# Macaron block on one core: the maxima's rows on another queue, the causal mask of the transposed scores without its own matmuls, and score units spread over a step

## The chip, the cores and the metric

One of the eight cores of a Trainium2 chip runs the whole program. A core has five engines with a queue each: PE (TensorE, matmuls into PSUM), DVE (VectorE), ACT (ScalarE), POOL (GpSimd) and SP, which only issues DMAs and waits. The metric is the device time of one execution in microseconds. The profile is of one execution; its span runs from the first to the last recorded instruction.

## What is computed

Four sequences of 256 tokens, 512 features, in float32. The block is half a feed-forward network, attention, and half a feed-forward network again:

```
x = x + 0.5 * ffn(layernorm(x))
x = x + attn(layernorm(x))
x = x + 0.5 * ffn(layernorm(x))

ffn:  h = silu(x @ w_gate) * (x @ w_up); h @ w_down        (width 1376, weights in 4 bits, scaled by group)
attn: qkv = x @ Wqkv                                        (32 heads of 16; one k and one v for all heads)
      scores = q k^T / 4 + slope[head] * (pos_k - pos_q)    (-1e30 where pos_k > pos_q)
      out = softmax(scores) @ v @ Wo
```

## The kernel before

All instructions are placed by hand, each engine's stream in a block of its own; a stream runs in the order in which it is written, and streams meet at semaphores. There is no scheduler. The program has these parts:

- **Stage A** (s = 0): weights are dequantised and half of the tokens goes through the first network, 11 column tiles j (`NJ`), for each `gate_up`, `silu`, `h_mul`, `h_high`/`h_low` and `down`. Matrices are split into a high and a low part, and three products stand for one.
- **Stage B** (s = 1): the other half of the tokens. Between its 11 tiles lies the preparation of attention: masks, tables and slopes on DVE (`partition_masks`, `tables`, `slope_table`, all in j = 0), the layer norm of the first half (`moments`, `rstds`, in j = 1), transposes on PE (in j = 2), and the projections of sequences 0 and 1.
- **Attention**: for each sequence b (a "step 0" to "step 3" below) 12 sub-steps n, which pair with the units of 8 heads in three forms, `o, u = divmod(n, 3)`. In sub-step n of b the kernel computes the transposed, shifted scores of b (`shifted_scores`, keys on partitions, banks 4 and 5), their exponentials on ACT (`exps`, into `pt` and `pt_far`), and sums with v one group later (`near_values`, `far_values`, then `even_heads` on ACT, `odd_heads` on DVE, `swap_sums` on PE, `normalise` on DVE). At the same time it computes plain scores of sequence b + 1 (`scores`, banks 6 and 7) for the maxima alone (`maxima` on DVE): `score_units` gives one unit to sub-steps 0 and 1, two to sub-step 2, and so on up to 8. A unit's scores wait until the unit before has been reduced. `between` holds what else lies in a sub-step: in steps 0 and 1 the layer norm, k, v and q of sequence b + 2, from step 1 on the output projection of b - 1, in step 3 the transposes for the last network.
- **Stage C and D** (s = 2, 3): the last network.

The operand `qp[b]` of both score products holds, per half s of the partitions, 64 rows: q's parts, the slopes and, in rows 18 and 19, the maxima with their sign turned, so that the matmul subtracts them. It is filled by DMA, all on SP's queue: `q_to_dram(b)` writes q to DRAM, `q_to_rows(b)` brings first the 16 slope rows (2 DMAs), then, once q has arrived in DRAM, q's rows (6 DMAs, semaphore `q_in[b]`), and `max_to_rows(b)` the maxima from the tile `two` (4 DMAs of 16 KB, semaphore `m_in[b]`). `shifted_scores(b, 0)` waits for `m_in[b]`, and `scores(b + 1, 0)`, the next thing in PE's stream, for `q_in[b + 1]`. The order on SP's queue is:

```
q_to_rows(1)
max_to_rows(0)
...
q_to_dram(2)
q_to_rows(2)
max_to_rows(1)
sp.wait_ge(a_st, 2 * NU)
q_to_dram(3)
q_to_rows(3)
max_to_rows(2)
max_to_rows(3)
```

Both score products get the causal mask from matmuls of their own, a product of an identity with a triangle of -1e30 in bfloat16, which opens the accumulation in the bank: L1337 for the plain scores, L1373 for the transposed ones (two per unit, 256 columns for u < 2 and 512 for u = 2). GpSimd does nothing once stage B has begun, but for one copy, which widens the slopes to `qp_a` (L542), and the making of `kconst`.

## Time and profile before

| | us |
|---|---|
| median of three runs | 712.94 (708.77 to 724.35) |
| profiled execution | 708.63, of which the span is 706.8 |
| PE busy | 605.2 (86%) |
| DVE busy | 326.1 (46%) |
| ACT busy | 158.9 (22%) |
| GpSimd busy | 47.8 (7%) |

The mean granted clock of TensorE is 0.925 of full speed. Busy shares are means over stages with different limits: the two networks keep PE busy nearly all the time, attention (from about 258 to 511 us) doesn't. A row `a [b <-ENGINE tile Lnnn]` of the timeline means that the engine sat idle b us before it, and what released it. `SPq` and `ACTq` are the DMA issues on those engines.

### The profile page before, as it was taken

How to read it: one execution, taken by the hardware profiler on the slowest of the kernel's cores; microseconds unless marked ns; L12 is line 12 of the kernel's file. 1: busy time of each engine (PE TensorE's matmuls, PEld its weight loads, DVE VectorE, ACT ScalarE, POOL GpSimd, SP SyncE). 2: the span in 40 equal slices, each digit the busy share in tenths (PEclk: the TensorE clock that was granted, in tenths of full speed). 3: DMA queues.
4: the chain of work that ended last, by engine and by line, in shares of the span. 5: the costliest groups of instructions: out<-in, count | busy, mean ns of one | idle time of the engine just before them, and what ended most of it. 6: DMA issues, size and time to landing. Idle time of an engine off the chain costs nothing.

```text
span 706.8 us, 7705 instructions
## 1 busy us (share of the span) xinstructions
PE 605.2 (86%) x3064; PEld 425.8 (60%) x3064; DVE 326.1 (46%) x641; ACT 158.9 (22%) x284; POOL 47.8 (7%) x59
## 2 busy tenths in 40 slices
PE   2499999979999978880798589868699999999998
PEld 1387777868776754540454233323367888788886
DVE  6798998633124455441255354554531124421113
ACT  1332323111111122230123222333411111211111
POOL 5683000003000000000000000000000000000000
PEclk9999999999999995995789968879899999999999
DMA  6587110961935400009003800000029100100001
GB/s 203 180 257 233 45 37 13 307 284 31 152 87 70 51 4 1 1 30 146 7 1 90 93 1 1 1 5 1 1 85 344 33 0 1 59 1 1 0 1 59
DMA packets 36956, 51.54 MB, mean 73 GB/s; under 512 B 10188, under 2 KB 27446, under 8 KB 36504
## 3 DMA queue, kind: packets, MB, share of 16 engines
q1 hardware_dynamic: 32592, 40.39, 24.1%
q0 software_dynamic: 2656, 10.57, 4.6%
...
## 4 chain that ended last, share of the span: by engine, by line
PE 59%; DVE 6%; DMA 4%; ACT 2%; SPq 2%; issue 1%; ACTq 0%
PE bank L1262 22%; PE bank L1280 10%; PE bank L1423 4%; PE bank L1312 4%; PE bank L1345 4%; PE bank L1395 3%; PE bank L1337 3%; PE bank L1381 3%; DVE nm L1032 2%; PE bank L1373 2%; PE bank L1416 2%; DMA qp_b<-two 2%; PE bank L1232 1%; DMA qp_c<-two 1%; SPq L424 1%
## 5 line engine op out<-in xcount | busy, mean ns | idle before, releaser
L1280 PE MATMUL bank<-w_d,hs 128*128 128x512 f32 (+1 forms) x528 | 129.2, 394 | 2.8 <-DVE hs L877 1.3
L1280 PEld LDWEIGHTS bank<-w_d,hs 128*128 128x128 f32 (+1 forms) x528 | 98.0, 188 | 26.8 <-issue 4.3
L1032 DVE TENSOR_REDUCE nm<-bank 128x2 f32<-128x512 f32 (+1 forms) x96 | 61.8, 686 | 109.9 <-PE bank L1345 109.9
L871 DVE TENSOR_TENSOR hf<-sil,bank 128x512 f32<-128x512 f32 (+1 forms) x44 | 30.2, 686 | 168.7 <-PE bank L1262 168.6
L1262 PE MATMUL bank<-xt,w_far 128*128 128x512 f32 (+1 forms) x384 | 92.5, 395 | 0.0
L1262 PE MATMUL bank<-xt,w_mid 128*128 128x512 f32 x384 | 91.7, 395 | 0.0
L1262 PEld LDWEIGHTS bank<-xt,w_mid 128*128 128x128 f32 x384 | 73.2, 191 | 15.4
L1262 PEld LDWEIGHTS bank<-xt,w_far 128*128 128x128 f32 (+1 forms) x384 | 69.3, 181 | 18.2
L1262 PE MATMUL bank<-xt,w_near 128*128 128x512 f32 x288 | 71.7, 405 | 9.4 <-issue 9.4
L1262 PEld LDWEIGHTS bank<-xt,w_near 128*128 128x128 f32 x288 | 55.4, 195 | 22.9 <-issue 10.7
L1373 PE MATMUL bank<-ident_b,causal 128*128 128x256 bf16 (+1 forms) x96 | 24.9, 347 | 40.5 <-DMA qp_b<-two 22.4
L604 ACT ACTIVATE sil<-bank 128x512 f32<-128x512 f32 (+1 forms) x44 | 26.3, 597 | 141.1 <-PE bank L1262 141.0
L612 ACT CAST hs<-hf 128x512 fp32r<-128x512 f32 (+1 forms) x44 | 27.3, 621 | 130.2 <-DVE hf L871 130.2
L1373 PEld LDWEIGHTS bank<-ident_b,causal 128*128 128x128 bf16 x96 | 8.4, 107 | 56.3 <-DMA qp_b<-two 22.7
L877 DVE TENSOR_TENSOR hs<-hf,hs 128x512 fp32r<-128x512 f32 (+1 forms) x44 | 32.9, 747 | 20.0 <-ACT hs L612 19.9
L1232 PE MATMUL bank<-ident,xn 128*128 128x128 f32 x96 | 17.0, 325 | 24.0 <-DVE xn L804 19.9
L1337 PE MATMUL bank<-causal,ident_b 128*128 128x256 bf16 (+1 forms) x96 | 25.1, 347 | 14.2 <-DVE nm L1032 13.4
L1312 PE MATMUL bank<-xa,wqkv 128*128 128x256 f32 x128 | 34.8, 428 | 0.0
L656 ACT ACTIVATE pt_a<-bank 128x512 f32<-128x512 f32 x32 | 17.4, 595 | 75.7 <-PE bank L1381 75.7
L1087 DVE RECIPROCAL den<-bank 128x256 f32<-128x256 f32 x16 | 28.0, 1753 | 13.6 <-PE bank L1416 13.6
L1232 PEld LDWEIGHTS bank<-ident,xn 128*128 128x128 f32 x96 | 13.1, 167 | 28.8 <-issue 19.1
L656 ACT ACTIVATE pt_b<-bank 128x512 f32<-128x512 f32 x32 | 17.4, 594 | 57.3 <-PE bank L1381 57.3
...
## 6 DMA issues: line engine op xcount, KB each, us to landing
...
```

Of the source, the lines that this page charges most:

```text
L656: nc.scalar.activation(dst, src, ACT.Exp).then_inc(a_exp, 1)
L871: nc.vector.tensor_tensor(hf[0:jw(jt(s, p)), n % 2, :], sil[0:jw(jt(s, p)), n % 2, :], up_ps[0:jw(jt(s, p)), :], ALU.mult).then_inc(h_ok, 1)
L877: nc.vector.tensor_tensor(hs[0:jw(jt(s, p)), n % 2, 1, :], hf[0:jw(jt(s, p)), n % 2, :], hs[0:jw(jt(s, p)), n % 2, 0, :].bitcast(F32), ALU ...
L1032: nc.vector.tensor_reduce(nm[:, min(u, 1), 2 * h0 + s:2 * (h0 + heads) + s - 1:2], bank[6 + s][:, :].rearrange("p (h n) -> p h n", h=heads ...
L1232: ins = nc.tensor.transpose(ps[:, k * P:(k + 1) * P], xn[:, n % 2, k * P:(k + 1) * P], ident[:, :])
L1262: ins = nc.tensor.matmul(ps[0:jw(j), :], w_gu(a, k, gu, j), xt[:, b, k, :], start=(k == 0 and q == 0), stop=(k == KT - 1 and q == 2))
L1280: ins = nc.tensor.matmul(acc[t][:, :], hs[0:jw(j), n % 2, a, t * P:(t + 1) * P], w_d[0:jw(j), j, b, :], start=(p == 0 and q == 0), stop=(p ...
L1312: ins = nc.tensor.matmul(q_bank(b, h)[:, m * S:(m + 1) * S], wqkv[:, k, (2 * h + m) * P:(2 * h + m + 1) * P], xa[:, k, :], start=(k == 0), ...
L1337: nc.tensor.matmul(ps[:, :, 4 * P // heads - P:], ident_b[:, :], causal[:, :].unsqueeze(1).to_broadcast([P, heads, P]), start=True, stop=F ...
L1345: ins = nc.tensor.matmul(bank[6 + s][:, i * w:(i + 1) * w], qp[b][rows, h, min(u, 1) * P:(min(u, 1) + 1) * P], kp[rows, b % 3, 0:w], start ...
L1373: nc.tensor.matmul(ps[:, :, 0:P], causal[:, :], ident_b[:, :].unsqueeze(1).to_broadcast([P, heads, P]), start=True, stop=False, skip_group ...
L1423: ins = nc.tensor.matmul(out_bank(b, t)[:, :], normed(b)[:, k, t * P:(t + 1) * P], wo[:, k, :], start=(k == 0), stop=(k == KT - 1))
```

## The change

- `max_to_rows` moves from SP's queue to ACT's. ACT issues the four DMAs for sequence b + 1 at the end of sub-step 11 of b, behind the exponentials and `even_heads` of that sub-step; those for sequence 0 right before attention.
- The mask matmuls L1373 of the transposed scores go. In their place the operands `kp` and `qp` get eight step functions of 32 positions in rows that were free (`key_steps`, `steps`, `kconst`, `slope_rows` 4 to 11), by which the product itself gets -1e30 for whole blocks of 32, and GpSimd sets the rest to zero behind the exponentials, with one `affine_select` per unit (512 elements per partition for u < 2, 1024 for u = 2). `near_values` and `far_values` wait for it (`a_sel`). The preparation gets longer by some GpSimd and DVE instructions, and four more DMAs to `slope_rows`.
- Where a sub-step has two units of plain scores, the second now comes behind `between` on PE, and on DVE behind `odd_heads` and `normalise`.
- In stage B `moments` and `rstds` come in j = 0, and masks and tables in j = 1 behind the first normalised tiles.
- A small exponential is put ahead of `max_high(0)`, and a small Silu behind the last exponentials.
- In step 2 and 3 the output projection moves one sub-step later, and in step 3 the transposes for stage C one earlier, into banks 6 and 7 instead of 0 and 1, without the wait for `a_x` 6.

```diff
@@ sync
-            def max_to_rows(b):
-                sp.wait_ge(a_mhi, b + 1)
...
             q_to_rows(1)
-            max_to_rows(0)
             sp.wait_ge(up_ok, 2 * NJ)
             q_to_dram(2)
             q_to_rows(2)
-            max_to_rows(1)
@@ gpsimd
+            for b in range(B):
+                for n in range(NU):
+                    o, u = divmod(n, 3)
+                    pool.wait_ge(a_exp, 2 * (NU * b + n) + 2)
+                    if u < 2:
+                        p = pt[o % 2][:, 2 * u:2 * u + 2, :, 0:P].rearrange("p h s q -> p (h s) q")
+                    else:
+                        p = pt_far[:, :, :, :].rearrange("p h s q -> p (h s) q")
+                    nc.gpsimd.affine_select(out=p, in_=p, compare_op=ALU.is_ge, fill=0.0, base=0,
+                                            pattern=[[0, 4 if u < 2 else 8], [1, P]],
+                                            channel_multiplier=-1).then_inc(a_sel, 1)
@@ scalar
+            def max_to_rows(b):
+                act.wait_ge(a_mhi, b + 1)
+                act.wait_ge(a_mlo, b + 1)
+                act.wait_ge(q_in[b], 16 * 8)
...
+                        act.dma_start(qp[b][64 * s + 18 + r:64 * s + 19 + r, :, :].bitcast(F32),
+                                      two[s:NH:2, r, :].bitcast(F32)).then_inc(m_in[b], 16)
...
-                if j == NJ - 1:
-                    max_high(0)
+            act.wait_ge(hot_ok, 1)
+            nc.scalar.activation(hot[:, 0:1], hot[:, 1:2], ACT.Exp)
+            max_high(0)
+            max_to_rows(0)
...
+                if n == 11 and b + 1 < B:
+                    max_to_rows(b + 1)
@@ vector
                 if j == 0:
-                    partition_masks()
-                    tables()
-                    slope_table()
-                if j == 1:
                     dve.wait_ge(x_upd, 4)
                     moments(range(4))
                     rstds(0)
@@ tensor, shifted_scores
-                for s in range(2):
-                    ps = bank[4 + s][:, :].rearrange("p (h q) -> p h q", h=heads)
-                    nc.tensor.matmul(ps[:, :, 0:P], causal[:, :], ident_b[:, :].unsqueeze(1).to_broadcast([P, heads, P]),
-                                     start=True, stop=False, skip_group_check=True)
@@ tensor, near_values
-                pe.wait_ge(a_exp, 2 * (3 * g + 2))
+                pe.wait_ge(a_sel, 3 * g + 2)
@@ tensor, between
-                first = 7 if b == 1 else 4
+                first = 7 if b == 1 else 5
...
-                if b == B - 1 and n in (8, 10):
-                    if n == 8:
-                        pe.wait_ge(a_x, 6)
-                    for t in range(n - 8, n - 6):
+                if b == B - 1 and n in (7, 9):
+                    for t in range(n - 7, n - 5):
                         ffn_transposes(2, t)
@@ tensor, attention loop
-                        for k in score_units(b + 1, n):
-                            scores(b + 1, k)
+                    units = score_units(b + 1, n) if (b, n) != (0, 0) else ()
+                    for k in units[0:1]:
+                        scores(b + 1, k)
...
                     between(b, n)
+                    for k in units[1:2]:
+                        scores(b + 1, k)
```

PE's stream at the end of step 0 and the start of step 1, before (L1373 is the mask of the transposed scores, L1381 their product, L1337 and L1345 mask and product of the plain scores, L1416 `swap_sums`, L1395 `near_values`):

```order
L1373 MATMUL bank<-ident_b,causal 128x2x128 [waits exp_done,max_rows_placed1]
L1373 MATMUL bank<-ident_b,causal 128x2x128
L1381 MATMUL bank<-qp_b,kp 128x512 x2
L1337 MATMUL bank_7<-causal,ident_b 128x512 [waits max_lo_ready,k_rows_ready,q_rows_placed2]
L1337 MATMUL bank_7<-causal,ident_b 128x512
L1345 MATMUL bank_7<-kp,qp_c 128x128 x8
L1416 MATMUL bank<-den,swap 128x256 [waits attn_normed,odd_heads_added]
L1395 MATMUL bank<-pt_b,vp 32x256 [waits odd_heads_added,exp_done]
```

The same place now (L1439 is the product of the transposed scores, L1399 and L1407 the plain scores, L1474 `swap_sums`, L1453 `near_values`):

```order
L1439 MATMUL bank<-qp_b,kp 128x512 [waits exp_done,max_rows_placed1]
L1439 MATMUL bank<-qp_b,kp 128x512
L1399 MATMUL bank_7<-causal,ident_b 128x512 [waits max_lo_ready,k_rows_ready,q_rows_placed2]
L1399 MATMUL bank_7<-causal,ident_b 128x512
L1407 MATMUL bank_7<-kp,qp_c 128x128 x8
L1474 MATMUL bank<-den,swap 128x256 [waits attn_normed,odd_heads_added]
L1453 MATMUL bank<-pt_b,vp 32x256 [waits odd_heads_added,exp_masked]
```

The two mask matmuls are gone; the wait for q's rows of sequence 2 stands where it stood, right behind the first transposed scores, and `near_values` waits for the select.

ACT's stream around the end of step 0, before (L656 `exps`, L642 `max_high`, L666 `even_heads`):

```order
L642 CAST two<-bank_7 32x256 [waits k_rows_ready,max_transposed]
L656 ACTIVATE pt_far<-bank 128x4x128 [waits shifted_scores_t_done,all_keys_times_v]
L656 ACTIVATE pt_far<-bank 128x4x128 [waits shifted_scores_t_done]
L666 ACTIVATE num<-bank,pmask 128x256 [waits sums_swapped,attn_normed,all_keys_times_v]
L666 ACTIVATE den<-bank,pmask 128x256
L656 ACTIVATE pt_a<-bank 128x2x256 [waits shifted_scores_t_done,first_keys_times_v]
```

And now (L690 `exps`, L666 `max_high`, L700 `even_heads`, L675 `max_to_rows`):

```order
L666 CAST two<-bank_7 32x256 [waits k_rows_ready,max_transposed]
L690 ACTIVATE pt_far<-bank 128x4x128 [waits shifted_scores_t_done,all_keys_times_v]
L690 ACTIVATE pt_far<-bank 128x4x128 [waits shifted_scores_t_done]
L700 ACTIVATE num<-bank,pmask 128x256 [waits sums_swapped,attn_normed,all_keys_times_v]
L700 ACTIVATE den<-bank,pmask 128x256
L675 DMA qp_b<-two 1x16x256 [waits q_rows_placed1,max_lo_ready,max_hi_ready]
L675 DMA qp_b<-two 1x16x256 x3
```

The four DMAs stand behind one sub-step's exponentials and copies, where SP issued them as soon as `two` was ready, but for what lay ahead of them on its own queue.

PE's stream in sub-step 2 of step 1, before (two units of plain scores one behind the other, then L1312, half of a q projection) and now (L1374 between them):

```order
L1337 MATMUL bank_7<-causal,ident_b 128x2x128 [waits max_ready]
L1337 MATMUL bank_7<-causal,ident_b 128x2x128
L1345 MATMUL bank_7<-kp,qp_c 128x256 x4
L1337 MATMUL bank_7<-causal,ident_b 128x512 [waits max_ready]
L1337 MATMUL bank_7<-causal,ident_b 128x512
L1345 MATMUL bank_7<-kp,qp_c 128x128 x8
L1312 MATMUL bank<-xa,wqkv 128x256 [waits attn_xt_ready]
L1312 MATMUL bank<-xa,wqkv 128x256 x3
```

```order
L1407 MATMUL bank_7<-kp,qp_c 128x256 x4
L1374 MATMUL bank<-xa,wqkv 128x256 [waits attn_xt_ready]
L1374 MATMUL bank<-xa,wqkv 128x256 x3
L1399 MATMUL bank_7<-causal,ident_b 128x512 [waits max_ready]
L1399 MATMUL bank_7<-causal,ident_b 128x512
L1407 MATMUL bank_7<-kp,qp_c 128x128 x8
```

The second unit moved behind the projection.

## Rows read from the trace of the kernel before

**Rows 1.** Windows over attention: length, busy time (count) of PE to POOL, clock, DMA share, GB/s.
```profile
257.70:326.50 68.80, 49.65 (x310) 28.62 (x309) 33.82 (x70) 18.93 (x37) 0.00 (x0) 0.77 0.15 31
...
340.20:399.35 59.15, 53.73 (x353) 29.69 (x352) 29.36 (x46) 16.88 (x35) 0.00 (x0) 0.90 0.28 46
...
406.50:461.75 55.25, 47.33 (x290) 20.26 (x290) 27.87 (x41) 15.73 (x33) 0.00 (x0) 0.78 0.01 1
461.75:511.30 49.55, 36.02 (x235) 15.68 (x235) 25.39 (x50) 19.57 (x39) 0.00 (x0) 0.84 0.01 2
```

**Rows 2.** Chain of waits between steps 0 and 1.
```profile
316.35 4.10 DMA q_rows<-qst
...
326.52 13.04 DMA qp_b<-two
...
340.94 0.54 PE bank L1337
```

**Rows 3.** Timeline of PE from the end of step 0: start, us, what, idle before it.
```profile
339.61 0.61 PE L1373 MATMUL bank<-ident_b,causal 128*128 128x256 bf16 x2 [22.36 <-DMA qp_b<-two]
...
356.39 1.03 PE L1337 MATMUL bank<-causal,ident_b 128*128 128x512 bf16 x2 [1.38 <-DVE nm L1032]
```

**Rows 4.** Windows where q's rows of sequences 2 and 3 end, columns as in rows 1.
```profile
337.00:337.50 0.50, 0.00 (x0) 0.00 (x0) 0.00 (x0) 0.00 (x0) 0.00 (x0) 0.50 0.34 29
...
404.00:404.50 0.50, 0.00 (x0) 0.00 (x0) 0.00 (x0) 0.00 (x0) 0.00 (x0) 0.50 0.48 39
```

**Rows 5.** Timeline of SP's queue.
```profile
315.95 0.84 SPq L402 DMA_DIRECT2D q_rows<-qst  x2
...
382.93 0.82 SPq L402 DMA_DIRECT2D q_rows<-qst  x2
```

**Rows 6.** Timeline of PE in steps 2 and 3.
```profile
407.77 1.04 PE L1337 MATMUL bank<-causal,ident_b 128*128 128x512 bf16 x2
...
453.23 1.22 PE L1416 MATMUL bank<-den,swap 128*128 128x256 f32 x2 [1.11 <-DVE den L1076]
...
495.55 1.85 PE L1232 MATMUL bank<-ident,xn 128*128 128x128 f32 x8 [3.47 <-DVE x L1094]
```

**Rows 7.** Chain of waits in step 2.
```profile
412.87 0.54 PE bank L1373 x2
...
461.75 2.17 DMA qp_a<-two
```

**Rows 8.** Timeline of ACT at the end of step 2.
```profile
461.70 0.49 ACT L666 ACTIVATE den<-bank,pmask 128x256 f32<-128x256 f32 x1
```

**Rows 9.** Chain of waits at the end of step 1.
```profile
390.53 0.22 PE bank L1373 x2
```

**Rows 10.** Chain of waits of step 3, its shares by line.
```profile
by line: PE bank L1395 13.3%; PE bank L1423 12.1%; PE bank L1381 10.5%; PE bank L1416 8.9%; PE bank L1373 8.6%; PE bank L1232 6.5%; issue 5.8%; ACT pt_far L656 5.8%; DMA qp_a<-two 4.6%; DVE den L1087 3.7%; DVE den L1076 3.6%; PE bank L1406 
```

**Rows 11.** Timeline of POOL.
```profile
1.54 0.29 POOL L467 TENSOR_SCALAR_AFFINE_SELECT ident<-ident 128x128 f32<-128x128 f32 x1 [0.16 <-POOL slope_in L465]
...
167.32 3.61 POOL L542 CAST qp_a<-slope_in 128x4096 fp32r<-128x4096 f32 x1 [44.66 <-PE bank L1262]
...
171.61 1.04 POOL L549 TENSOR_SCALAR kconst<-kconst,pmask 128x256 f32<-128x256 f32 x1
```

**Rows 12.** Timeline of DVE in stage B, j = 3 and 4.
```profile
168.23 3.25 DVE L877 TENSOR_TENSOR hs<-hf,hs 128x512 fp32r<-128x512 f32 x1 [0.69 <-ACT hs L612]
...
181.47 0.69 DVE L877 TENSOR_TENSOR hs<-hf,hs 128x512 fp32r<-128x512 f32 x1 [0.69 <-ACT hs L612]
```

**Rows 13.** Timeline of PE in stage B, j = 2.
```profile
139.67 2.88 PE L1262 MATMUL bank<-xt,w_mid 128*128 128x512 f32 x12
146.29 1.06 PE L1232 MATMUL bank<-ident,xn 128*128 128x128 f32 x8 [3.74 <-DVE xn L804]
147.12 4.58 PE L1262 MATMUL bank<-xt,w_mid 128*128 128x512 f32 x12
```

**Rows 14.** Chain of waits at the start of attention: start, us, what.
```profile
262.71 1.28 ACT L656
```

100 lines of the change are left out of this document (72 added, 28 removed).

## The prediction

> **What bounds the kernel now.** I read the page first (which engine is busy, and in which slices), then the windows over attention, then the chain of waits inside each step, and last the timelines of single engines around each wait. In the two networks PE runs nearly without a gap, and the change hardly touches them. In attention it doesn't: in its four steps PE is busy 49.7, 53.7, 47.3 and 36.0 us of 68.8, 59.2, 55.3 and 49.6 [rows 1], and the granted clock is 0.77 to 0.90, a mix of the two levels 1.2 and 2.4 GHz. Inside a step the chain runs mostly through PE; between steps it runs through a DMA. The largest wait of the program is there: between steps 0 and 1 q goes to DRAM in 4.10 us, SP issues q's rows, and the maxima's rows, four small DMAs behind them on the same queue, take 13.04 us to land, until 339.56 [rows 2]. PE waits 22.4 us for them [rows 3], and again at the same place between steps 1 and 2.
>
> **The change part by part.**
>
> *Maxima's rows on ACT's queue.* This looks like it could give back these waits. It can't, because of what PE does next. Right behind the first transposed scores its stream has the plain scores of the next sequence, which wait for all of q's rows, and this wait has stayed in its place. Those rows move as long as the DMA engines are busy, to about 337.4, and in the next gap to about 404.3 [rows 4]. SP started with them at 315.95 and 382.93 [rows 5], so they arrive 21.4 us later. Before, PE reached those plain scores at 340.94 and 407.77 [rows 2, 6], which is 25.0 and 24.8 us behind the same starts. The gain is 25.0 - 21.4 = 3.6 and 24.8 - 21.4 = 3.4; I take 0.3 off each for the maxima's 64 KB in between, and count 3.3 + 3.1 = 6.4 us. The first transposed scores then lie inside the wait. As the lag of 21.4 us starts at the last q of the step, whatever makes the step faster behind that point (sub-steps 10 and 11 of step 0, 7 to 11 of step 1) is worth nothing.
>
> Between steps 2 and 3 there is no q, and the same edit costs. The last DMA left SP at 461.75 and took 2.17 us [rows 7]. On ACT all four come behind the last exponentials and a copy that ends at 462.19 [rows 8]; with about 0.6 us for each of three issues ahead of it (the lag of SP's own, estimated) the last leaves at 464.0 and lands at 466.1 instead of 463.9: 2.2 later, of which the missing mask matmul returns 0.3. Cost 1.9 us. Ahead of step 0 ACT is idle, and nothing changes.
>
> The Trainium skill ("DMA: Bandwidth & Descriptors", "Issuing engines are not separate DMA queues") says that a second issuing engine saves little more than issue time, since all transfers run on the same 16 DMA engines; its section on queues and rings says that each engine takes turns between the queues it has work for. By the first, the maxima's rows would land with q's rows and the 6.4 us would be gone (a rival below); by the second they overtake. No row here shows two queues at once.
>
> *Mask matmuls gone.* There are 96. What counts is their part of the chain: a pair with 256 columns is 0.22 us there at full clock [rows 9], so 0.43 with 512, and 0.54 at half clock [rows 7]. In step 0 four pairs are on the path ahead of the last q (sub-steps 4, 5, 7, 8): 0.22 + 0.43 + 0.22 + 0.43 = 1.3; the first three sub-steps wait for DVE. In step 1 there are four as well (1, 2, 4, 5): 1.3, and some of it at half clock, 1.6. In step 2 sub-steps 1, 2, 4 and 10 stand at half clock, 5, 7 and 8 at full: 0.54 + 0.5 + 0.54 + 0.43 + 0.43 + 0.22 + 0.43 = 3.1. In step 3, where PE waits for exponentials and these for the masked scores, they are 8.6% of the chain's 47.4 us [rows 10], 4.1.
>
> *Select on GpSimd.* The nearest row is a select of 128 elements in 0.29 us [rows 11]; with 0.1 as its fixed part, 512 elements take 0.9 and 1024 take 1.6, or 3.4 us per group of three sub-steps, which last 10 to 14. By the slowest rate in sight, 1.04 us for 256 elements [rows 11], it is 2.1 and 4.2, 8.4 per group. Both fit, and `near_values` and `far_values` come a sub-step or more behind the exponentials, some 4 to 5 us; so I price the wait at nothing, with that cover. It can touch DVE: beside the copy L542 on GpSimd a DVE subtraction took 3.25 us, and 0.69 without it [rows 12]. In attention one DVE instruction per group, the product in `normalise`, has two SBUF operands, and step 3 has some more. It follows `swap_sums` and a reciprocal, when the select has mostly ended. I take 2 us in all; the bound is 16 groups by 1.6, 26 us. The Trainium skill ("SBUF — State Buffer", "SBUF: two separate sides") calls this port pair an exclusive lock, held for the whole instruction; the trace agrees [rows 12].
>
> *Two units spread.* Before, a sub-step with two units had a wait of 1.38 us between them [rows 3]. Now the other work lies there, but the next sub-step's unit waits in turn for the second one's maximum, 1.3 us, of which only 0.45 is covered by transposed scores. So of 1.38 + 0.75 (the next transposed scores with their mask) there remain 1.3: a gain of 0.8 where `between` is filled. In step 0 that is sub-step 5 (0.8) and sub-step 8, behind which no unit comes: 1.7. In step 1 sub-steps 2 and 5: 1.6. In step 2 sub-step 5: 0.8, and sub-step 8, where the output projection moves in from sub-step 4 and also covers the 1.11 us at 453.23 [rows 6]: 1.38 + 0.75 + 1.11 - 0.43 = 2.8.
>
> *Stage B.* PE waits 3.74 us for the first normalised tiles and then runs 12 matmuls in 4.58 us instead of 2.88, since the clock fell [rows 13]. With `moments` and `rstds` (5.4 us on DVE) in j = 0 the tiles are ready at about 142.1, when PE needs them at 142.4. Masks, tables and `key_steps` then hold DVE to about 148, 2 us longer than the next `h_mul` wants; PE has `down` and `gate_up` in that time and doesn't wait. Gain 3.7 + 1.7 = 5.4. The longer preparation on GpSimd and SP (about 3 us) has 9 to 12 us to spare until the first plain scores.
>
> *Small exponential.* The table load of 1.28 us [rows 14] leaves the chain, and a little of DVE's queue with it: 1.6.
>
> *Step 3.* The wait of 3.47 us for `a_x` [rows 6] goes, and the output projection fills the gap; so PE reaches everything behind sub-step 8 that much earlier. The transposes, a sub-step earlier in both places, no longer stand between the last exponentials and the last normalised tiles, which is worth about 1 us more by the order of the streams. I take 4.4: with the masks' 4.1 that is 8.5.
>
> The sum: 5.4 (stage B) + 1.6 (table) + 1.3 + 0.8 + 1.7 (step 0) + 3.3 (gap) + 1.6 + 1.6 (step 1) + 3.1 (gap) + 3.1 + 0.8 + 2.8 - 1.9 (step 2) + 8.5 (step 3) - 2 (DVE beside GpSimd) = 31.7 us. The profiled execution took 708.6 (span 706.8), so it would take 677. It stands 0.6% below the median of the three runs (712.9) and with their lowest; I forecast 679, a little above the sum for that reason. A change of under 2%, some 14 us, is what a measurement of this kernel can't tell from none.
>
> **The rivals.**
>
> 1. *The maxima's rows don't overtake.* They land with q's rows, at 339.6 in terms of before. Then the two gaps give nothing: 679 + 6.4 = 685. For it: the same 16 DMA engines are full at that time. Against: 64 KB in all, issued 4 us before q's rows leave.
> 2. *The gaps close.* If q's rows were not what PE waits for next, 16 to 20 us more would go: 661. Against it: the order of PE's stream.
> 3. *GpSimd in the way.* Selects at the slow rate, and DVE's two-operand instructions behind them in every group, about 1 us for each of 16 on the path: 695.
> 4. *The clock falls* (the slower side). With the mask matmuls gone PE works less densely in attention, and 1.2 GHz may hold where 2.4 was granted. By [rows 1] (clock c means a share of 2c - 1 at full) about 121 us of PE's work in attention ran at full clock; each microsecond of it turned to half costs one more. From 32 us, a quarter of it, the gain is gone; with 40% it is 679 + 48 = 727. For it: the clock fell behind each wait of some 4 us [rows 13]. Against: the masks are a small part of PE's 187 us in the four steps, and several waits go too.
>
> **How the numbers follow.** Forecast 60%, its own range 665 to 690 (masks and waits 5 either way, the clock 8). Rival 1 12%, rival 2 6%, rival 3 13%, rival 4 9%. The range from 664 to 697 leaves out rival 4, rival 2 and the tails. Faster by over 2% means below 698.7: 0.85; within 2%: 0.09; slower: 0.06.
>
> **What would show it.** In the profile after: PE waits for q's rows, not the maxima's, at the plain scores (some 20 us, then 7); the wait ahead of step 3 is 5 to 6 us instead of 3.7; no wait at the transposes of j = 2; selects of 0.9 and 1.6 us; a granted clock of about 0.8 in the steps. The prediction is wrong if the gap between steps 0 and 1 shrinks by much more than 4 us, if `near_values` or `far_values` wait for GpSimd, or if the clock is below 0.7 in steps 1 to 3.

## The result and the profile after

| | before | after |
|---|---|---|
| median | 711.57 us (4 runs, 708.77 to 724.35) | 671.86 us (4 runs, 669.77 to 672.79) |
| profiled execution | 708.63 us, span 706.8 | 672.25 us, span 670.2 |
| PE busy | 605.2 us | 575.2 us |
| GpSimd busy | 47.8 us | 89.0 us |

Each execution is in one of two states, a faster and, rarely, a slower one (724.35 is such a run), and the ratios, and from here on the medians, are of those in the faster state. The ratio is 0.945, with a 95% interval of 0.9405 to 0.9495: 38 us faster (710.19 to 671.86), where 34 were forecast (712.94 to 679). All of it lies ahead of the last network. First the page of the changed kernel, busy time and slices:

```profile
PE 575.2 (86%) x2968; PEld 413.3 (62%) x2968; DVE 327.3 (49%) x647; ACT 159.2 (24%) x286; POOL 89.0 (13%) x113
...
PE   1499999999999996890599479678899999999998
...
PEclk9999999999999997895689779969799999999999
DMA  7579110591592800009203800000097000100001
```

The two slices in which PE falls to 0 and 4 tenths while DMA is at 9 and 8 are the gaps between steps 0, 1 and 2. They are still there. The changed kernel in windows, with the columns of [rows 1]: step 0 to the store of the last q, gap, step 1, gap (step 1's last sub-steps lie beside it), step 2 with the wait behind it, step 3, last network:

```profile
256.47:301.17 44.70, 36.84 (x268) 22.14 (x268) 30.68 (x65) 15.84 (x32) 8.02 (x11) 0.85 0.00 1
301.17:324.56 23.39, 1.01 (x5) 0.29 (x3) 2.12 (x5) 2.90 (x6) 2.09 (x3) 0.54 0.93 137
324.56:362.94 38.38, 35.26 (x257) 21.57 (x258) 21.75 (x35) 11.27 (x23) 5.37 (x7) 0.88 0.00 1
...
386.41:433.57 47.16, 37.24 (x266) 17.02 (x266) 28.66 (x43) 16.18 (x33) 9.47 (x12) 0.86 0.01 2
433.57:473.85 40.28, 31.86 (x210) 13.66 (x211) 25.25 (x48) 19.16 (x38) 9.47 (x12) 0.80 0.00 1
473.85:670.20 196.35, 192.55 (x846) 153.74 (x842) 50.50 (x89) 29.79 (x50) 0.00 (x0) 0.99 0.17 53
```

The same stretches of the kernel before:

```profile
261.81:315.95 54.14, 45.76 (x288) 26.53 (x288) 30.46 (x64) 16.68 (x32) 0.00 (x0) 0.78 0.00 1
315.95:340.87 24.92, 2.30 (x9) 0.72 (x9) 2.20 (x5) 2.25 (x6) 0.00 (x0) 0.55 0.85 130
340.87:382.93 42.06, 38.43 (x273) 23.23 (x272) 21.70 (x35) 12.35 (x25) 0.00 (x0) 0.86 0.00 1
...
407.77:463.96 56.19, 46.06 (x288) 19.84 (x287) 28.75 (x43) 16.17 (x33) 0.00 (x0) 0.77 0.01 2
```

Cut at the same events (first transposed scores, SP's store of q, first plain scores of the next step), the two traces give this account. "Forecast" is the prediction's own terms.

| stretch | before | after | gain | forecast |
|---|---|---|---|---|
| start to the first transposed scores | 261.8 | 256.5 | 5.3 | 5.4 |
| step 0 (with the table load) | 54.1 | 44.7 | 9.4 | 5.4 |
| gap 0/1 | 24.9 | 23.4 | 1.5 | 3.3 |
| step 1, to the store of q | 42.1 | 38.4 | 3.7 | 3.2 |
| gap 1/2 | 24.8 | 24.2 | 0.6 | 3.1 |
| step 2, to the first product of step 3 | 56.2 | 46.4 | 9.8 | 4.8 |
| step 3 | 47.3 | 40.3 | 7.0 | 8.5 |
| last network | 195.5 | 196.4 | -0.8 | 0 |
| DVE beside GpSimd | | | | -2 |
| sum | 706.8 | 670.2 | 36.6 | 31.7 |

Two things stand out: the steps 0 and 2 gained about twice what I summed, and the gaps, for which the change of queue was made to count, a third. For step 0 a part of this can be chance: its code took up to 2.6 us longer in other traces of kernels that share it (below), and the kernel before has one trace. PE's timeline in gap 0/1, beside [rows 3], and at the start of step 2 and of step 3:

```profile
312.09 0.80 PE L1439 MATMUL bank<-qp_b,kp 64*128 64x512 f32 x2 [10.71 <-DMA qp_b<-two]
324.56 1.03 PE L1399 MATMUL bank<-causal,ident_b 128*128 128x512 bf16 x2 [11.67 <-DMA qp_c<-q_rows]
...
386.41 0.79 PE L1439 MATMUL bank<-qp_c,kp 64*128 64x512 f32 x2 [10.82 <-DMA qp_c<-two]
...
433.57 0.79 PE L1439 MATMUL bank<-qp_a,kp 64*128 64x512 f32 x2 [4.89 <-DMA qp_a<-two]
```

In gap 0/1 the one wait of 22.36 us became two, 10.71 and 11.67, and their sum is the same. The chain of waits in the two gaps has the transfers (start, us, what):

```profile
301.55 4.73 DMA q_rows<-qst
...
308.53 15.98 DMA qp_c<-q_rows
...
377.76 8.60 DMA qp_c<-two
```

The store of q took 4.73 us beside the maxima's rows on ACT's queue, 4.10 without them [rows 2]; that they were the reason is not shown, since in gap 1/2, where no maxima moved yet, SP went on to the query rows 5.07 us behind the store, and 5.13 in gap 0/1. The last 16 KB of maxima left ACT at 377.76 and needed 8.60 us in gap 1/2; at the end of step 2, with nothing beside them, 2.17 [rows 7]. ACT's own timeline shows that it sent them in good time in gap 0/1.:

```profile
301.74 0.54 ACTq L675 DMA_DIRECT2D qp_b<-two  x1
...
303.10 1.50 ACTq L675 DMA_DIRECT2D qp_b<-two  x2
```

In gap 1/2 it sends the first only at 375.94, 13 us behind the store, since the sub-steps of step 1 that finish the maxima come behind the one with the last q.

The selects on GpSimd, the new work, take 0.64 and 1.09 us where I took 0.9 and 1.6. PE's weight loads for `near_values` and `far_values` are recorded waiting for one three times, 1.1 us in all; first two of the selects, then the wait of `near_values` (us, times, longest):

```profile
258.23 0.64 POOL L572 TENSOR_SCALAR_AFFINE_SELECT pt_a<-pt_a 128x512 f32<-128x512 f32 x1 [87.68 <-ACT pt_a L690]
...
261.85 1.09 POOL L572 TENSOR_SCALAR_AFFINE_SELECT pt_far<-pt_far 128x1024 f32<-128x1024 f32 x1 [1.33 <-ACT pt_far L690]
...
PEld bank L1453 <- POOL pt_b L572: 0.9, 2, 0.7
```

In stage B the transposes of j = 2 follow the products without a wait (3.74 us before, [rows 13]), and those products keep their rate:

```profile
140.07 2.89 PE L1324 MATMUL bank<-xt,w_mid 128*128 128x512 f32 x12
142.80 1.03 PE L1294 MATMUL bank<-ident,xn 128*128 128x128 f32 x8
143.59 2.75 PE L1324 MATMUL bank<-xt,w_mid 128*128 128x512 f32 x11
```

### The profile page after: what moved, and what is told of

The parts are those of the page before. It is cut to its first block, busy times and chain, and to the rows that moved or that the text cites. A ratio compares the mean times of both kernels' runs of the same rounds, so it can differ in the third digit from the quotient of the medians.

```text
span 670.2 us, 7580 instructions
## 1 busy us (share of the span) xinstructions
PE 575.2 (86%) x2968; PEld 413.3 (62%) x2968; DVE 327.3 (49%) x647; ACT 159.2 (24%) x286; POOL 89.0 (13%) x113
## 4 chain that ended last, share of the span: by engine, by line
PE 58%; DVE 6%; DMA 5%; ACT 3%; issue 1%; SPq 0%; ACTq 0%; DVEq 0%
PE bank L1324 23%; PE bank L1342 11%; PE bank L1481 4%; PE bank L1407 4%; PE bank L1374 3%; PE bank L1453 3%; PE bank L1399 3%; DMA qp_c<-q_rows 2%; DVE nm L1086 2%; PE bank L1439 2%; PE bank L1474 2%; DMA qp_c<-two 1%; PE bank L1294 1%; PE bank L1355 1%; DVE x L925 1%
## 5 line engine op out<-in xcount | busy, mean ns | idle before, releaser
L1086 DVE TENSOR_REDUCE nm<-bank 128x2 f32<-128x512 f32 (+1 forms) x96 | 61.8, 685 | 93.6 <-PE bank L1407 93.6
L1324 PE MATMUL bank<-xt,w_mid 128*128 128x512 f32 x384 | 90.1, 390 | 0.0
L1324 PE MATMUL bank<-xt,w_near 128*128 128x512 f32 x288 | 73.4, 412 | 9.4 <-issue 9.4
L1324 PEld LDWEIGHTS bank<-xt,w_near 128*128 128x128 f32 x288 | 56.5, 199 | 23.5 <-issue 10.8
L1399 PE MATMUL bank<-causal,ident_b 128*128 128x256 bf16 (+1 forms) x96 | 24.5, 341 | 24.1 <-DVE nm L1086 11.8
L690 ACT ACTIVATE pt_a<-bank 128x512 f32<-128x512 f32 x32 | 17.4, 594 | 76.2 <-PE bank L1439 76.2
L572 POOL TENSOR_SCALAR_AFFINE_SELECT pt_a<-pt_a 128x512 f32<-128x512 f32 x16 | 10.2, 638 | 168.0 <-ACT pt_a L690 168.0
L1374 PE MATMUL bank<-xa,wqkv 128*128 128x256 f32 x128 | 30.8, 390 | 0.0
L1399 PEld LDWEIGHTS bank<-causal,ident_b 128*128 128x128 bf16 x96 | 6.2, 99 | 38.5 <-DVE nm L1086 16.4
L690 ACT ACTIVATE pt_b<-bank 128x512 f32<-128x512 f32 x32 | 17.4, 598 | 43.5 <-PE bank L1439 43.5
L1374 PEld LDWEIGHTS bank<-xa,wqkv 128*128 128x128 f32 x128 | 24.0, 193 | 5.1 <-issue 1.6
## 6 DMA issues: line engine op xcount, KB each, us to landing
qp_a<-q_rows SPq DMA_DIRECT2D x12, 256.0 KB, 11.3
raw_d<-in_L_ffn_qweight_down SPq DMA_DIRECT2D x10, 256.0 KB
x<-in_L_attn_hidden_states SPq DMA_DIRECT2D x8, 256.0 KB, 3.6
```

Source lines behind the costliest of these rows:

```text
L690: nc.scalar.activation(dst, src, ACT.Exp).then_inc(a_exp, 1)
L1086: nc.vector.tensor_reduce(nm[:, min(u, 1), 2 * h0 + s:2 * (h0 + heads) + s - 1:2], bank[6 + s][:, :].rearrange("p (h n) -> p h n", h=heads ...
L1324: ins = nc.tensor.matmul(ps[0:jw(j), :], w_gu(a, k, gu, j), xt[:, b, k, :], start=(k == 0 and q == 0), stop=(k == KT - 1 and q == 2))
L1374: ins = nc.tensor.matmul(q_bank(b, h)[:, m * S:(m + 1) * S], wqkv[:, k, (2 * h + m) * P:(2 * h + m + 1) * P], xa[:, k, :], start=(k == 0), ...
L1399: nc.tensor.matmul(ps[:, :, 4 * P // heads - P:], ident_b[:, :], causal[:, :].unsqueeze(1).to_broadcast([P, heads, P]), start=True, stop=F ...
```

## The experiments

What a run says is read from its trace first. Medians of one kernel on other occasions move by more than some of these terms: the kernel before stood at 705.1 to 710.2 us, with single runs from 702.5 to 712.9. The trace of *units late* below shows one source: in its first 60 us PE lost 8 us of work, and attention began 12 us later. Its edit lies in attention only, and the two last versions, which have it too, began attention at 254.5 and 256.0 us, as the changed kernel did (256.5). So each run is compared by the stretches of the table above, and its ratio to before is given too. "From the first scores" is the span from the first transposed scores to the end: 413.7 us in the changed kernel, 445.0 before.

Step 2 (first to next transposed scores behind a DMA wait, 47.16 us) is the steadiest of them: five other traces in which nothing in it was edited, but for the maxima's queue in one, have 46.7, 47.2, 47.2, 47.3 and 46.9. Step 0 is not: with the same code it took 44.5 to 47.3 in eight of the runs below, at granted clocks of 0.85 for most of the short ones, 0.81 for two of 45.6 and 45.7, and 0.78 for the two of 47.3. Step 1 behind its gap took 37.1 to 38.6, and step 3 40.0 to 41.3.

### 1. Maxima's rows on SP's queue again

```diff
-                if n == 11 and b + 1 < B:
-                    max_to_rows(b + 1)          # on ACT
+            q_to_rows(2)
+            max_to_rows(1)                      # on SP, as before, for each b
```

Expected:

> The changed kernel with one part undone: the rows of maxima are issued on SP's queue again, behind the next sequence's query rows; all else as changed. The changed kernel measured 671.9 us (0.945 of before). Theory A (what was saved in the gaps is small, because the 16 KB of maxima on ACT's queue share the DMA engines with the 2 to 3 MB of queries on SP's): the gaps 0/1 and 1/2 get longer by 1 to 3 us each, the gap 2/3, where nothing else moves, by nothing or less (the ACT issues of 1.8 us go), in all +1 to +6 us: 673 to 678 us. Rival B (the queue brought most of the surplus over the forecast, since the units of the next sequence start earlier): +12 to +17 us, 684 to 689 us. What the trace should show under A: PE's wait for two of gap 0/1 nearly as long as in the kernel before (13 us), and the start of each next step later by that alone.

Measured: 670.38 us, ratio 0.9501 (0.9431 to 0.9572); from the first scores 414.1 us. PE's timeline in gap 0/1:

```profile
324.06 0.80 PE L1439 MATMUL bank<-qp_b,kp 64*128 64x512 f32 x2 [23.40 <-DMA qp_b<-two]
324.79 1.04 PE L1399 MATMUL bank<-causal,ident_b 128*128 128x512 bf16 x2
```

SP stored q at 300.45, so both operands were there 23.6 us later. In the changed kernel it is 324.56 - 301.17 = 23.4, and in the kernel before 339.61 - 315.95 = 23.7 for the maxima's rows. In gap 1/2 it is 386.41 - 362.94 = 23.5 after, 23.7 here, 23.6 before. Whichever queue sends them and whichever lands first, the last of all these rows lands 23.4 to 23.7 us after the store began. Neither range is met: nothing was lost by going back (-1.5 us by the medians, +0.4 from the first scores), where theory A had +1 to +6 and 1 to 3 us in each gap. A is right only in that the queue brings little. Rival B (+12 to +17) is out. What gap 0/1 gained in place, 1.5 us, is 0.5 for the mask products that stood before the transposed scores and about 1 for the scores themselves, now inside the wait; the latter is not to be found in the end (step 1 behind it took 38.4 us, here 37.1, at granted clocks of 0.88 and 0.91). The cost that I put on gap 2/3 isn't there either: 46.7 us for step 2 here, 47.2 after, 0.5 instead of 1.9.

### 2. Mask products back

```diff
+                    nc.tensor.matmul(ps[:, :, 0:P], causal[:, :], ident_b[...], start=True, stop=False)   # s = 0, 1
-                    nc.tensor.matmul(..., w, q, start=True, stop=True)
+                    nc.tensor.matmul(..., w, q, start=False, stop=True)
```

> The changed kernel with the two mask products of each transposed unit put back before the score products (they add the causal mask in PSUM once more; the spare contraction rows and the select on GpSimd stay, so the mask is there twice). Theory A (the masks cost the path what I summed for them: 1.3 + 1.6 + 3.1 + 4.1 us): +10 us, 682 us. Theory B (their removal also raised the granted clock of the steps, which is where steps 0 and 2 gained 4 to 5 us each more than I summed): +14 to +20 us, 686 to 692 us, with the granted clock of steps 0 to 2 back at 0.78 to 0.82 instead of 0.85, 0.88, 0.86. Theory C (the masks lay in PE's waits for ACT and DVE in any case): under +5 us.

Measured: 680.38 us, ratio 0.9663 (0.9574 to 0.9752); from the first scores 421.9 us, +8.2. Its windows of steps 0, 1, 2 and 3:

```profile
256.70:303.82 47.12, 41.42 (x288) 23.78 (x288) 31.33 (x64) 15.40 (x31) 7.89 (x10) 0.86 0.00 1
...
327.05:364.64 37.59, 35.48 (x271) 21.60 (x272) 21.63 (x35) 11.27 (x23) 5.38 (x7) 0.94 0.00 1
388.08:438.50 50.42, 42.24 (x290) 18.78 (x290) 28.74 (x43) 16.18 (x33) 9.44 (x12) 0.87 0.01 3
438.50:482.53 44.03, 36.85 (x234) 15.40 (x234) 25.23 (x48) 19.27 (x38) 9.45 (x12) 0.81 0.00 1
```

Against the changed kernel's trace the masks cost 2.4, -0.8, 3.3 and 3.8 us, where I had 1.3, 1.6, 3.1 and 4.1. So theory A holds, 8 to 9 us instead of 10, well shown for steps 2 and 3. For step 0 it is 1.4 to 2.6 against the traces at its clock (0.85, 44.5 to 45.8 us), and nothing against the two long ones of 47.3. Theory B falls on the clock column: with the masks back the granted clock is no lower (0.86, 0.94, 0.87, 0.81 against 0.85, 0.88, 0.86, 0.80). The masks were not what held steps 0 and 2 at 0.78 before. In step 1 no cost can be told: 37.6 us lies among the 37.1 to 38.6 of the traces without masks. The clock was higher in this one (0.94 against 0.88 to 0.91); whether the products themselves raised it is open.

### 3. Units together again

```diff
-                    for k in units[0:1]:
+                    for k in units:
                         scores(b + 1, k)
                     between(b, n)
-                    for k in units[1:2]:
-                        scores(b + 1, k)
```

> The changed kernel with both score units of a sub-step together again, ahead of the products between, as before the change. Theory A (the spread saves the wait at the head of each double, 7 doubles of about 1 us in steps 0 to 2): +6 to +8 us, 678 to 680 us; the waits of 2.9 to 3.7 us on the nm of DVE at doubles come back. Rival B (the wait only moves from the first unit to the second): within 2 us, 670 to 674 us. Rival C (spreading is what removed the surplus of steps 0 and 2): +12 to +16 us, 684 to 688 us.

Measured: 685.89 us, ratio 0.9718 (0.965 to 0.9786); from the first scores 425.0 us, +11.3. Its windows of steps 0 and 2:

```profile
254.25:303.88 49.63, 40.52 (x266) 23.66 (x266) 30.67 (x64) 15.61 (x32) 7.72 (x10) 0.79 0.00 1
...
390.96:442.92 51.96, 40.80 (x268) 18.00 (x268) 28.74 (x43) 16.18 (x33) 9.44 (x12) 0.80 0.01 2
```

Step 2 is 4.8 us longer, and of these 40.80 - 37.24 = 3.6 are the same products taking longer, at a granted clock of 0.80 instead of 0.86. Only 1.2 are waits. Step 0 is 4.9 longer (2.3 to 5.1 against all traces of its code), again mostly in PE's busy time. The median is 14 us up, in rival C's range, and the trace 11.3, between theory A's 6 to 8 and C's 12 to 16: the spread units are worth some 11 us, and they are where step 2, and step 0 as far as its own spread allows, passed the forecast. Rival B is out.

### 4. Idle products in the gaps

```diff
+            def warm_up(b, count):
+                pe.wait_ge(a_mlo, b + 1)
+                for _ in range(count):
+                    nc.tensor.matmul(bank[7], ident_b, ident_b ...)      # 128x512, bf16
...
+                    if b >= 1: warm_up(b, (38, 38, 14)[b - 1])   # before the wait for m_in[b]
+                    if b >= 2: warm_up(b - 1, (40, 0)[b - 2])    # before the wait for q_in[b]
```

> The changed kernel with 38, 38 and 14 idle products (identity, 512 columns, into a bank that is free then) in front of the wait for the rows of maxima of sequences 1, 2 and 3, and 40 in front of the wait for the query rows of sequence 2: PE works in the gaps instead of waiting, the results are not used. If the granted clock at the start of each step is low because PE waited before it, steps 1, 2 and 3 start at the higher level and the time falls by 2 to 5 us: 667 to 670 us. If the work before has no say (or costs clock later): 672 us or more, up to 676 where the idle products outlast the waits. Either way the starts on SP and the ends of the waits move by under 1 us.

Measured: 665.28 us, ratio 0.9417 (0.9352 to 0.9483). The rows still landed 23.5 us after the store (303.51 to 327.03). Step 1 behind that point, and step 2:

```profile
327.03:361.24 34.21, 31.08 (x257) 19.90 (x258) 21.73 (x35) 11.27 (x23) 5.35 (x7) 1.00 0.00 1
384.91:430.10 45.19, 38.06 (x280) 17.61 (x281) 28.55 (x43) 16.18 (x33) 9.52 (x12) 0.92 0.01 3
```

The same instructions of step 1 took 34.2 us instead of 38.4, at full clock throughout instead of 0.88, and step 2 and 3 gained 2.0 and 1.1. The first plain scores show it product by product: 0.61 us for the pair here, 1.03 after the wait. This is the one experiment in which nothing changed but what PE did while it waited, so it shows the link outright: a gap in PE's work costs its length, and then slower products behind it, here 3 to 4 us behind gap 0/1 (34.2 against 37.1 to 38.6 in all traces of this code), about 2 behind gap 1/2 and 1 behind step 2. Step 0, ahead of any idle product, took 47.3 us at 0.78 in this trace, one of the long ones, so that from the first scores it shows only 2.4 us less; the median shows 6.6.

### 5. Order of stage B back

```diff
                 if j == 0:
-                    dve.wait_ge(x_upd, 4); moments(range(4)); rstds(0)
+                    partition_masks(); key_steps(); tables(); slope_table()
                 if j == 1:
+                    dve.wait_ge(x_upd, 4); moments(range(4)); rstds(0)
                     xn_tile(...)                # t = 0, 1
-                    partition_masks(); key_steps(); tables(); slope_table()
```

> The changed kernel with the order on DVE in the first stage put back: masks, key steps and tables before the moments and the first normalised tiles. Theory A (PE's first transposes and with them the query projections wait for DVE): +4.5 to +5.5 us, 677 us, with the first projection of queries back at 157.0 from 151.9 us. Rival B (the stage is bound by the weights' arrival, the 5.1 us seen are made up later in the gaps, whose length is set by the DMA): +0 to +2 us, 672 to 674 us.

Measured: 682.67 us, ratio 0.9687 (0.9599 to 0.9775); from the first scores 413.4 us, as after. PE's timeline in j = 2:

```profile
146.92 1.94 PE L1294 MATMUL bank<-ident,xn 128*128 128x128 f32 x8 [4.49 <-DVE xn L843]
148.51 4.73 PE L1324 MATMUL bank<-xt,w_mid 128*128 128x512 f32 x12
```

The wait and the slow products of [rows 13] are back, both a little larger with `key_steps` ahead of them. The first transposed scores came at 263.1 instead of 256.5, 6.7 us later, and nothing of it was made up later. Theory A holds, with a somewhat larger size; rival B is out. The median went up by 10.8 us, more than the trace; its single runs spread over 10 us (678.2 to 688.2).

### 6. Sub-steps of the output projection and of the last transposes back

```diff
-                first = 7 if b == 1 else 5
+                first = 7 if b == 1 else 4
-                if b == B - 1 and n in (7, 9):
+                if b == B - 1 and n in (8, 10):
+                    if n == 8: pe.wait_ge(a_x, 6)
```

(and `attn_out`, `xt_high`, `xt_low` and `ffn_xn` with them, and the transposes' banks 0 and 1)

> The changed kernel with the sub-steps of the output projection, of attn_out and of the tiles' transposes in steps 2 and 3 put back where they were. Theory A (step 3's gain was 4.4 us of such waits and step 2 lost 1.9 us nothing by it): +3 to +5 us, 675 to 677 us, all of it from the start of the last step's units to the end. Rival B (the masks and the clock gave step 3 its gain): within 1.5 us.

Measured: 681.19 us, ratio 0.9681 (0.9601 to 0.9761); from the first scores 420.2 us, +6.5, so more than theory A's 3 to 5, and far beyond rival B's 1.5. Step 3 is 4.1 us longer (44.37 instead of 40.28; forecast 4.4), with the wait of 3.47 us of [rows 6] back to the digit and another behind it:

```profile
466.20 1.76 PE L1294 MATMUL bank<-ident,xn 128*128 128x128 f32 x8 [3.47 <-DVE x L1150]
...
474.07 1.30 PE L1294 MATMUL bank<-ident,xn 128*128 128x128 f32 x8 [2.21 <-DVE xn L843]
```

Step 2 is 3.2 us longer too, which neither theory had:

```profile
386.94:437.32 50.38, 39.72 (x266) 17.96 (x267) 28.64 (x43) 16.18 (x33) 9.51 (x12) 0.80 0.01 2
```

2.5 of these 3.2 are again PE's busy time, at 0.80 instead of 0.86.

### 7. No early table loads

```diff
-            nc.scalar.activation(hot[:, 0:1], hot[:, 1:2], ACT.Exp)
...
-            nc.scalar.activation(hot[:, 0:1], hot[:, 1:2], ACT.Silu)
```

> The changed kernel without the two idle activations on ACT that bring in the tables of Exp and Silu early. Theory A (a table load of 1.28 us each at the first use, one of which PE waits for at the first transposed scores): +1.3 to +1.6 us, 673.3 us. Rival B (it lies under another wait): 0, 671.9 us. At 0.2% of the time the trace decides more than the ratio: the wait in front of the first Exp.

Measured: 673.39 us, ratio 0.9552 (0.9491 to 0.9612); from the first scores 413.4 us. ACT and PE at the first exponential:

```profile
256.27 1.28 ACT L690 ACT_TABLE_LOAD   x1 [5.24 <-PE bank L1436]
```

```profile
258.71 0.49 PE L1436 MATMUL bank<-qp_a,kp 64*128 64x512 f32 x2 [2.51 <-ACT pt_a L690]
```

PE's wait for the second unit is 2.51 us instead of 1.23: 1.3 us in its place, as theory A has it. In the whole it can't be seen: step 0 took 45.8 us, within what the same code takes. The second activation, for Silu, shows nothing (last network 194.9 us, 196.4 after).

### 8. Selects cut to one element

This kernel leaves out the diagonal part of the causal mask and prices the selects.

```diff
+                    p = p[:, 0:1, 0:1]
                     nc.gpsimd.affine_select(out=p, in_=p, ..., pattern=[[0, 1], [1, 1]], ...)
```

> The changed kernel with each of the 48 selects on GpSimd cut to one element per partition: the diagonal part of the causal mask is left out, all waits and the order stay. It prices what the selects cost, which I put at 2 us beside DVE and nothing else. Theory A (no engine waits for them and DVE's two-operand products are seldom beside them): 0 to -1 us, 671 to 672 us, and the four steps within 1 us of the changed kernel's. Rival B (they delay near_values and far_values, or DVE): -2 to -5 us, 667 to 670 us, with shorter waits in step 3, where the exponentials bind.

Measured: 670.70 us, ratio 0.9491 (0.9433 to 0.9549); from the first scores 412.8 us, -0.9; step 2 46.9 and step 3 40.6 (after: 47.2 and 40.3). The medians differ by 1.2 us. Theory A: the 38 us of selects in the four steps cost about 1 us, about as much as the 1.1 us for which PE's weight loads waited for them, and which this trace has not. My 2 us for DVE were too much.

### 9. Units of sequence 2 later

```diff
         def score_units(b, n):
+            if b == 2:
+                return range(NU)[max(0, 12 * (n - 2) // 7):max(0, min(NU, 12 * (n - 1) // 7))]
```

> The changed kernel with the 12 score units of sequence 2 taken from sub-step 2 of step 1 on instead of from sub-step 0: the sub-steps 0 and 1 hold only products of their own, so that PE has work while the query rows of sequence 2 land. The changed kernel waits 11.7 us there (L1399 on qp_c<-q_rows at 324.56). Theory A (it is that wait alone, the work in front covers it): -8 to -12 us, 660 to 664 us. Rival B (the units pressed together cost doubles, 5 of 12, and the queries of sequence 3 on SP wait for the last unit): -2 to -5 us, 667 to 670 us. Rival C (the maxima and their rows come later, and the wait moves to gap 1/2): 0 to +3 us.

Measured: 671.44 us (664.66 to 673.31), ratio 0.9505 (0.9437 to 0.9573); from the first scores 402.6 us, -11.1. By the time of the whole it is no faster than the changed kernel (671.86): three of its four executions took 671 to 673 us. What follows is read from one trace, whose start shows where the gain went in that execution; the other three have no trace. Its profiled execution is the one in which attention began 12 us later, and the window of the first 60 us shows it in both kernels; after, then this one:

```profile
0.00:60.00 60.00, 36.92 (x148) 29.82 (x149) 46.65 (x98) 17.30 (x23) 40.73 (x53) 1.00 0.72 222
```

```profile
0.00:60.00 60.00, 28.78 (x99) 21.43 (x99) 39.32 (x89) 14.16 (x18) 38.64 (x54) 0.94 0.71 216
```

In its attention the second wait of gap 0/1 is gone. PE runs on with its own sub-steps while the query rows land, and meets the plain scores at 338.51 without one:

```profile
324.80 0.79 PE L1441 MATMUL bank<-qp_b,kp 64*128 64x512 f32 x2 [10.81 <-DMA qp_b<-two]
...
338.51 0.61 PE L1401 MATMUL bank<-causal,ident_b 128*128 128x512 bf16 x2
```

From q's store of sequence 2 to that of sequence 3 it took 51.6 us instead of 61.8: 10.1 us, theory A. That the gain is real in the whole kernel too is borne out by experiment 11, which has this edit and adds up. Here the other queue may matter: the maxima's rows land at 11 us, while q's rows still move. That it is worth those 10 us together with this edit is an inference; the edit with the maxima on SP's queue was not run.

### 10. Slope rows of sequences 2 and 3 early

```diff
             sp.wait_ge(up_ok, 2 * NJ)
+            slopes_to_rows(2)
             q_to_dram(2)
             q_to_rows(2)                # without its slope rows
             sp.wait_ge(a_st, 2 * NU)
+            slopes_to_rows(3)
             q_to_dram(3)
```

> The changed kernel with the two DMAs of slope rows of sequences 2 and 3 (a quarter of the rows that each buffer gets) sent ahead of the wait for the last queries, so that in the gap only the query rows move. From SP's start to the plain scores that wait for the rows the changed kernel takes 23.4 us in gap 0/1 and 24.2 us in gap 1/2 (there the maxima's rows, on ACT's queue, come last). Theory A (the 16 DMA engines are full from the queries' store to the last row, so bytes count): a quarter of about 17 us less, 4 us in each gap, in all -6 to -9 us, 663 to 666 us, and the maxima's rows land sooner too. Rival B (the six DMAs of query rows have a rate of their own by their rows' length, and the slopes fill what they leave): under 1.5 us in each gap, 669 to 671 us.

Measured: 666.93 us, ratio 0.9438 (0.938 to 0.9495); from the first scores 410.7 us, -3.0, with step 0 at its long 47.3. PE's timeline in the gaps:

```profile
308.22 0.79 PE L1447 MATMUL bank<-qp_b,kp 64*128 64x512 f32 x2 [4.80 <-DMA qp_b<-two]
323.43 1.03 PE L1407 MATMUL bank<-causal,ident_b 128*128 128x512 bf16 x2 [14.41 <-DMA qp_c<-q_rows]
```

SP stored q at 303.20 and 361.70, so the query rows were there after 20.2 us instead of 23.4, and in gap 1/2 PE started after 21.4 instead of 23.5. Theory A in direction, with 3.2 and 2.1 us for the 4 that I expected in each, and 4.9 us by the medians for its 6 to 9. The maxima's rows landed 5.0 us behind the store, 10.9 in the changed kernel. In gap 0/1 as many bytes still moved, since SP sent the slope rows of sequence 3 at 309.99, right behind the query rows; what helped is that the query rows no longer stood behind slopes. Sending those of sequence 3 later was not run.

### 11 and 12. Versions with the three edits

The first has experiments 9 and 10 and idle products (20, 20, 14) together; the second moves the units of sequence 2 to sub-step 3 and has 20, 26 and 19, and 8 ahead of the query rows.

```diff
+                return range(NU)[max(0, 12 * (n - 2) // 7):max(0, min(NU, 12 * (n - 1) // 7))]      # first, b == 2
+                return range(NU)[max(0, 2 * (n - 3)):max(0, min(NU, 2 * (n - 2)))]                  # second, b == 2
```

> Three edits together on the changed kernel: score units of sequence 2 from sub-step 2 of step 1 on (-10.3 us in its own trace), idle products in front of the waits for the maxima's rows (20, 20 and 14; -7.1 us over steps 1 to 3 with 38, 38, 14 and 40), slope rows early. If they add up, with idle products worth some 4 us where less of the gap is left, and slopes worth nothing in gap 0/1 since the plain scores no longer wait there but about 4 us in each maxima's wait: 671.9 - 10.3 - 4 - 6 = 651.6; range 650 to 657 us. If the early slopes bring nothing: 657 us. If the idle products in the gap only helped through the 40 in front of the plain scores: 655 to 661 us.

Measured: 652.92 us (650.56 to 653.81), ratio 0.9252 (0.9197 to 0.9307), 19 us below the changed kernel: the three add up to what was summed, 651.6. The windows of step 0, the stretch from q's store of sequence 2 to that of 3, step 2 and step 3:

```profile
254.52:299.02 44.50, 36.95 (x268) 22.12 (x268) 30.64 (x65) 15.84 (x32) 7.98 (x11) 0.85 0.00 1
299.02:347.02 48.00, 36.30 (x254) 22.11 (x252) 22.47 (x37) 14.16 (x29) 7.46 (x10) 0.89 0.39 68
369.26:414.43 45.17, 37.92 (x280) 17.22 (x280) 28.56 (x43) 16.16 (x33) 9.52 (x12) 0.92 0.01 3
414.43:453.68 39.25, 31.26 (x211) 13.41 (x211) 25.58 (x48) 19.14 (x38) 9.46 (x12) 0.83 0.00 1
```

The second of them took 61.8 us in the changed kernel. What remains in it is PE waiting 5.36 us at the first plain scores:

```profile
319.32 1.01 PE L1418 MATMUL bank<-causal,ident_b 128*128 128x512 bf16 x2 [5.36 <-issue]
```

The row names no releaser. It starts 20.3 us behind q's store, where in experiment 10 the query rows had landed (20.2), so I take it that they end this wait.

> The version with three edits (652.9 us, span 648.8 in its trace), with two things set by what its trace left: the units of sequence 2 from sub-step 3 of step 1 on, two in each of six sub-steps, since PE still waited 5.4 us for the query rows at the first unit in sub-step 2; and 20, 26 and 19 idle products ahead of the three waits for the maxima's rows (2.0 and 1.5 us were left in the last two), with 8 in front of the query rows. If the units' place costs nothing, the wait at the query rows falls from 5.4 to about 2 us and the rest gains 1 us of clock: 647 to 650 us. If six doubles in a row cost as the missing spread did (11.3 us for 16 units in three steps, about 1.2 us for each double behind it): 3 to 5 more doubles take back 4 to 6 us: 652 to 656 us.

Measured: 654.25 us (650.17 to 656.47), ratio 0.9265 (0.9206 to 0.9324); from the first scores 395.8 us, 394.3 in the first version. The wait at the query rows fell to 1.82 us and the stretch to 46.4 us, 1.6 less, but the 26 idle products now end after the maxima's rows have landed, and from the store to the first scores of step 2 it takes 370.83 - 347.70 = 23.1 us instead of 22.2. The median lies in the second range (652 to 656), but its reason is not shown: from the first scores this version is 1.5 us longer than the first, with 0.8 in step 0, whose code is the same, 0.9 in the gap and 1.2 in step 2, and the stretch with the doubles is the one that got shorter. The first version is the one to keep.

## Why the prediction was right, and where its steps were off

The total (679 for 672) and the sign were right, and most terms held. Undone one by one, the parts cost 0.4 (queue), 8.2 (masks), 11.3 (spread), 6.7 (stage B), 6.5 (sub-steps) and 1.3 us (table, in its place) in the traces, 34.4 of the 36.6 gained, where the sum had 31.7. That the total came so close is in part luck: behind it stand two errors of opposite sign, the gaps (6.4 summed, 2.1 gained) and the spread units with the clock behind them.

*Stage B* (5.4): right. 5.3 between the two traces, 6.7 in the undoing. *Table load* (1.6): 1.3 in its place; too small to see in the whole.

*Maxima's rows on ACT's queue* (6.4 in the gaps, minus 1.9 at the end of step 2): mis-sized, and the one step whose reasoning failed. "So they arrive 21.4 us later" was read off the moment when the DMA engines' share fell, and took that moment for the landing. PE could start 23.4 us behind the store of q, and in the kernel before the maxima's rows, which came last, were there at 23.7. In gap 0/1 of the changed kernel the share fell 21.3 to 21.8 us behind the store, as foreseen, and the rows were there another 1.5 to 2.2 us later, at 324.51:

```profile
322.50:323.00 0.50, 0.00 (x0) 0.00 (x0) 0.00 (x0) 0.00 (x0) 0.00 (x0) 0.50 0.29 25
323.00:323.50 0.50, 0.00 (x0) 0.00 (x0) 0.00 (x0) 0.00 (x0) 0.00 (x0) 0.50 0.03 0
```

The same lag stands in the kernel before, where the share fell at about 337.4 [rows 4] and the maxima's rows were there at 339.56 [rows 2]. These 2 us, which I left out of each gap, are most of the 4.3 us missing from the two. Query rows and maxima's rows are parts of one batch that keeps the engines 0.93 busy from the store on; putting 64 KB at its head rather than its end moved them forward by nearly 13 us (10.9 instead of 23.7 behind the store), and the end of the batch by 0.2 to 0.3. Undone, the edit changed nothing that can be measured. In gap 1/2 even the maxima's rows came last, at 386.37, nearly 2 us after the traffic had died down:

```profile
384.50:385.00 0.50, 0.00 (x0) 0.00 (x0) 0.00 (x0) 0.00 (x0) 0.00 (x0) 0.50 0.03 2
```

So rival 1, which I gave 12%, had the right price and half of the mechanism: the rows do overtake in one gap, and it is worth nothing. The sentence of the Trainium skill that I weighed ("DMA: Bandwidth & Descriptors", "Issuing engines are not separate DMA queues": a second issuing engine saves only the time on the sequencer) describes the end of both gaps better than my lag did; the trace agrees with it there, at 23.4 to 23.7 us from store to last row on either queue.

*Rival 2* (the gaps close if PE had something else to do next) described a kernel that could be built: experiment 9 made PE's stream have it, and 10 of the 16 to 20 us went.

*Mask matmuls* (1.3 + 1.6 + 3.1 + 4.1): 2.4, -0.8, 3.3 and 3.8 measured, 8 to 9 in all. Counting pairs on the chain by their duration there was sound for steps 2 and 3; in step 1, where the granted clock was higher with the masks than without, no cost can be told.

*Two units spread* (0.8 and 1.7 in step 0, 1.6, and 0.8 and 2.8 in step 2): this is the term that was most off, 7.7 (the 2.8 with the output projection's move in it) against 11.3 in the trace for the units alone and 3.2 more in step 2 for the move. What I left out is what a shorter wait does to the products around it: of the 4.8 us that the units brought in step 2 only 1.2 were waits. There the same products took 37.2 us of PE's time at a granted clock of 0.86, and 40.8 with the units together at 0.80. The kernel before had 0.77 there. In step 0 the same reading holds less firmly, as one code ran there at 0.85 and at 0.78. Rival 4 spoke of the clock, but with the opposite sign: it asked whether less work would lower it, and not whether fewer waits would raise it. That the waits come first and the clock follows is shown by experiment 4, where only the content of the waits changed; that the spread works by the same link is read from the clock column of experiment 3, not shown apart from it.

*GpSimd* (2 us, and rival 3 with 13%): about 1 us. The selects took 0.64 and 1.09 us, below the lower of my two estimates. "I price the wait at nothing" was off by 1.1 us: `near_values` and `far_values` did wait for GpSimd, three times, which by my own list of signs would have counted against the prediction.

*Step 3* (4.1 + 4.4 = 8.5): the terms alone measured 3.8 and 4.1; together 7.0, at a granted clock of 0.80 against 0.86 before.

*The other signs.* I had put PE's waits at the plain scores at some 20 and 7 us. In gap 0/1 the wait was split, 10.71 for the maxima's rows and 11.67 for q's, and in gap 1/2 PE waited 10.82 us for the maxima's rows and not at all for q's. The wait ahead of step 3 was 4.89 us for 5 to 6, the waits at the transposes of j = 2 were gone, and the clock stood at 0.80 to 0.88 in the steps.
